# The memory's first update moved beside the scores, and sixteen more periods with keys, then values, then queries

## The chip, the cores and the metric

The kernel runs on one core of one Trainium2 chip. The metric is the device time of one execution in microseconds; the number given for a kernel is the median of its runs.

## What is computed

x has shape (4, 512, 512), the side input the same, the condition (4, 128). The reference is two residual stages, each behind a bidirectional decayed scan:

```python
y = bi_wkv(x, side, side, w, u, cond)            # scans along the 512 tokens, forward and back
q, k, v = y @ Wq, y @ Wk, y @ Wv                 # 16 heads of 128
for each segment of 128 tokens:                  # 4 segments, state (mem, z) per head
    scores = q k^T / sqrt(128), causal; att_dot = softmax(scores) @ v
    sq, sk = elu(q) + 1, elu(k) + 1
    att_mem = sq @ mem / (sq @ z)
    delta = v - sk @ mem / (sk @ z)
    mem += sk^T @ delta ; z += sum(sk)
    att = beta * att_mem + (1 - beta) * att_dot
x = x + att @ Wo
x = x + fwht(silu(z @ W1^T) * (z @ W3^T)) @ W2^T # z = bi_wkv(x, ...) again
```

The change touches the attention alone.

## The kernel before, in words

The program is one core's, with the order of the work of each engine written out by hand. The projections are float32r matmuls in three terms (high times high, high times low, low times high; the helper `three`, L666 to L668), a step of 512 columns each. The weights' high and low halves lie in a ring of seven slots of `parts` (1 MB a tile, both halves together). The small matmuls and transposes of the attention are plain float32, which the trace shows as two passes each for the 128-column ones of L817, L834, L842, L843 and L862.

The attention runs in 32 periods n = 0 to 31: sample n // 8, pair of heads n % 8. A period computes the attention of its two heads and, between those small steps, the projections for the next period: keys k and queries q of n + 1 (`kq_part`, two head halves j, two parts each), and values v (`v_block`, two token halves, two parts each). Values of a couple of head pairs are computed over two periods. Every fourth period (4, 8, ... 28), a burst, has the output projection `wo` of four periods in it besides.

TensorE's order in an ordinary period n: `turn_k` (transposes of sk, L805), `scores` (L817), `turn_att` of n - 1 (L871), two parts of values into bank G[0], `update(n, 0)` (first update of the memory, L834, into a third of bank Z), values into G[1], `recall(n, 1)` (L842, L843), keys, `turn_p` (L852), `update(n, 1)`, keys, `recall(n, 2)`, `pv` (L862), keys, `update(n, 2)`, queries, `recall(n, 3)`, queries. Period 6 alone (`SWAPPED`) has keys where the others have values, values in the middle and queries last.

ScalarE empties the banks G: `copy_v` (L1914) for values; `copy_kq` (L1880), `relu_kq` (L1898) and `minus_exp` (L1889) for keys and queries. The next block into the same bank waits for the semaphore of the last reader: a_v (value copy), a_km (relu of keys) or a_qm (relu of queries). It also has the softmax exponentials (`exp_s`, L1928), `copy_pt` (L1936) and the copy of kn (L1921). VectorE adds the update to the memory (`memory`, L1322), makes delta, the joins and sigma. GpSimd scales the values (`scale_v`, L2299). The second scans and the Hadamard transform of W2 lie between these steps, in `behind(n, k)`, eight places a period, shared out by costs; HH (L1796) and HO (L1814) are ScalarE's part of the transform.

SyncE loads the weights in the order of `STREAM`, which `weight_stream` builds; a tile goes into the next slot of the ring and its load waits until the tile before in that slot has been used (`wait_used`). `held` keeps the slots of a couple's values until the odd period's part of the list has passed. `PLACE` maps a tile's name to its place in the list, `value_tiles` and `kq_part` find their tiles by it. In an even period that is no burst the values of a couple are loaded once and serve the next period too; behind a burst they are loaded again under the kind w. `fetch_x` loads the next sample's x (xb, four transfers) in periods 10, 18 and 26.

Of the kernel before, what the change touches and what calls it, by code (L numbers as in the profile page):

```python
# [19 lines left out]
NN = NB * NG  # L20
# [69 lines left out]
def is_burst(n):  # L90
    return n % 4 == 0 and n > 0
# [60 lines left out]
RAW = [("k", 0), ("v", 0), ("q", 0), ("v", 1)]  # L152


SWAPPED = 6


def couple(n):

    return n + 2 - n % 2  # L160
# [11 lines left out]
def weight_stream():  # L172
    stream, ends = [], []
    for n in range(NN - 1):
        a = couple(n)
        values = [(value_kind(n), a), (value_kind(n), a + 1)]
        has = a < NN and (n % 2 == 0 or is_burst(n - 1))
        keys = [("k", n + 1), ("q", n + 1)]
        if n == 0:
            stream += keys + values  # L180
        elif n == SWAPPED:
            stream += keys[:1] + values + keys[1:]
        else:
            if has:
                stream += values
            if is_burst(n):
                stream += [("o", 8 * (n // 4 - 1) + i) for i in range(8)]
            stream += keys
        ends.append(len(stream))
    ends.append(len(stream) + 3)  # L190
    stream += [("1", 0), ("3", 0)] + [("o", 8 * 7 + i) for i in range(8)] + [("2", 0)]
    for g in range(1, 2 * NG):
        stream += [("1", g), ("3", g), ("2", g)]
    return stream, ends
# [118 lines left out]
def adaln_attn_ffn(nc, xT_d, fT_d, wu_d, wq_d, wk_d, wv_d, wo_d, betas_d,  # L313
# [9 lines left out]
    with ExitStack() as ctx:  # L323
# [338 lines left out]
        def tensor(e):  # L662
# [56 lines left out]
            def v_block(n, half, part):  # L719
                i, k = value_tiles(n)  # L720
                if part == 0:
                    wait_split(w, i)
                    wait_split(w, k)
                    wait_y(couple(n) // NG)
                    if n == 0:
                        w.wait_ge(a_qm, 2 + half + 1)
                    elif n == 1:
                        w.wait_ge(a_v, 2 + blocks_by(0, half))
                    elif n == SWAPPED:
                        w.wait_ge(a_km, 2 * (n + 1) + half + 1)  # L730
                    else:
                        w.wait_ge(a_qm, 2 * n + half + 1)
                b = couple(n) // NG
                rows = slice(128 * tokens_of(n, half), 128 * tokens_of(n, half) + 128)
                x, y = SLOT[i], SLOT[k]
                for c in (0, 1) if part == 0 else (2, 3):
                    hi, lo = (parts[:, p, x:y + 1:y - x, 256 * c:256 * c + 256] for p in range(2))
                    m = three(G[half][:, :], yh[b % 2][:, c, rows], yl[b % 2][:, c, rows], hi, lo, c == 0, c == NC - 1)
                if part == 1:
                    m.then_inc(pe_v, 1)  # L740

            def kq_part(n, kind, j, part):
                b, i = n // NG, PLACE[kind, n]
                hi, lo = ring(i)
                if part == 0:
                    wait_split(w, i)
                    if kind == "q" and n - 1 == SWAPPED:
                        w.wait_ge(a_v, 2 + blocks_by(n - 1, j))
                    elif kind == "q":
                        w.wait_ge(a_km, 2 * n + j + 1)  # L750
                    elif is_burst(n - 1):
                        w.wait_ge(v_xb, 4 * ((n - 1) // 4 - 1) + j + 3)
                    elif n - 1 == SWAPPED or n == NN - 1:
                        w.wait_ge(a_qm, 2 * (n - 1) + j + 1)
                    elif n > 1:
                        w.wait_ge(a_v, 2 + blocks_by(n - 1, j))
                    if n == 1:
                        w.wait_ge(v_v, j + 1)
                        wait_y(0)
                for c in (0, 1) if part == 0 else (2, 3):  # L760
                    cols = slice(256 * c + 128 * j, 256 * c + 128 * j + 128)
                    m = three(G[j][:, :], hi[:, cols], lo[:, cols], yh[b % 2][:, c, :], yl[b % 2][:, c, :],
                              c == 0, c == NC - 1)
                if part == 1:
                    m.then_inc(pe_k if kind == "k" else pe_q, 1)
# [152 lines left out]
            for n in range(NN):  # L918
# [3 lines left out]
                scores(n)  # L922
                if n > 0:
                    turn_att(n - 1)
                bare = n in (0, NN - 2)
                if n in (SWAPPED, NN - 2):
                    kq_part(nx, "k", 0, 0)
                    kq_part(nx, "k", 0, 1)
                elif more and not bare:
                    v_block(n, 0, 0)  # L930
                    v_block(n, 0, 1)
                elif not more:
                    w.wait_ge(a_qm, 2 * n + 2)
                    up(0, 0, "1", G[0])
                if n == 0:
                    kq_part(nx, "k", 0, 0)
                update(n, 0)
                behind(n, 1)
                if more:
                    if n in (SWAPPED, NN - 2):  # L940
                        kq_part(nx, "k", 1, 0)
                    elif not bare:
                        v_block(n, 1, 0)
                    if burst:
                        v_block(n, 1, 1)
                else:
                    up(0, 0, "3", G[1])
# [2 lines left out]
                    behind(n, 3)  # L950
                if burst:
                    wo(n // 4 - 1, 0)
                elif n == SWAPPED:
                    kq_part(nx, "k", 1, 1)
                    v_block(n, 0, 0)
                elif more:
                    if not bare:
                        v_block(n, 1, 1)
                    if n < NN - 2:
                        kq_part(nx, "k", 0, 1 if bare else 0)  # L960
# [6 lines left out]
                if burst:  # L967
                    wo(n // 4 - 1, 1)
                elif bare:
                    kq_part(nx, "k", 1, 0 if n == 0 else 1)  # L970
                elif n == SWAPPED:
                    v_block(n, 0, 1)
                elif more:
                    kq_part(nx, "k", 0, 1)
                else:
                    w.wait_ge(v_f1, 1)
                    up(0, 1, "1", G[0])
                recall(n, 2)
                pv(n)
                if burst:  # L980
                    wo(n // 4 - 1, 2)
                    wo(n // 4 - 1, 3)
                elif n == SWAPPED:
                    v_block(n, 1, 0)
                    v_block(n, 1, 1)
                elif more:
# [718 lines left out]
        def scalar(e):  # L1705
# [311 lines left out]
            for n in range(NN):  # L2017
# [21 lines left out]
                    split_hi(o + 2 if burst else end + 1 if n == 3 else end - 1 if more else end)  # L2039
                exp_s(n, 1)  # L2040
                behind(n, 1)
                if n in (SWAPPED, NN - 2):
                    behind(n, 2)
                    copy_kq(nx, "k", 0, G[0])
                    exp_kq(nx, "k", 0, G[0])
# [9 lines left out]
                    copy_v(n, 1)  # L2055
                split_hi(o + 3 if burst else 3 if n == 0 else end if more else end + 1)
                behind(n, 3)
                if n == SWAPPED:
                    copy_kq(nx, "k", 1, G[1])
                    exp_kq(nx, "k", 1, G[1])  # L2060
                elif more and not bare and not burst:
# [11 lines left out]
                if burst:  # L2073
                    split_hi(o + 8)
                elif more:
                    if n == SWAPPED:
                        copy_v(n, 0)
                    elif n < NN - 2:
                        copy_kq(nx, "k", 0, G[0])
# [2 lines left out]
                behind(n, 5)  # L2082
                if burst:
                    split_hi(end)
                elif n == SWAPPED:
                    copy_v(n, 1)
                elif more:
                    copy_kq(nx, "k", 1, G[1])
# [608 lines left out]
```

## Time and profile before

| | us |
|---|---|
| median of 3 runs | 1576.99 (1576.73 to 1577.36) |
| the profiled execution | 1576.35 |
| its span | 1574.5 |
| TensorE busy | 1540.2 (98%) |
| VectorE busy | 1228.3 (78%) |
| ScalarE busy | 781.2 (50%) |
| GpSimd busy | 613.7 (39%) |
| bytes moved by DMA | 276.58 MB |

The span is the time from the first to the last instruction of the profiled execution; what lies around it is 1.85 us. The granted clock of TensorE was 0.998 over the execution. Periods are told by the first matmul of L805: period 9 starts at 344.17 us, 10 at 370.27, 11 at 396.37, 12 at 422.53, 18 at 623.69 and 25 at 852.04. A time of day in a row is in us from the span's start. Matmuls overlap, so the price of a group is read from start to start, not from the durations. A DMA is issued on SyncE's queue (SPq) and lands later; the time to landing counts from the issue.

### The profile page before, as it was taken

Reading aid. Unit: us, or ns where it says so; the run is one execution under the profiler, and the core shown is the slowest. Engines: PE = TensorE matmul, PEld = TensorE weight load, DVE = VectorE, ACT = ScalarE, POOL = GpSimd, SP = SyncE. Lnnn points to the kernel's source line nnn. Section 1 sums busy time; section 2 is a strip of 40 time slices with the busy share of each in tenths; the row PEclk is TensorE's granted clock in tenths of the full one; section 3 lists DMA queues with packets and bytes.
Section 4 is the critical chain, followed back from the end, with each engine's and each line's share of the span. In section 5 each row is a group of like instructions: output and inputs, shape, how many; then the busy total and the mean of one; then the engine's idle time right before and its main releaser. Section 6 shows DMA issues by size and latency. Waiting matters only on the chain.

```text
span 1574.5 us, 24552 instructions
## 1 busy us (share of the span) xinstructions
PE 1540.2 (98%) x8406; PEld 1321.9 (84%) x8406; DVE 1228.3 (78%) x2746; ACT 781.2 (50%) x1687; POOL 613.7 (39%) x433
## 2 busy tenths in 40 slices
PE   4999999999999999999999999999999999999999
PEld 2788988888888888888888888888888888888887
DVE  8879968898888788898765764776897888677785
ACT  3566656545625526544555562663554443444442
POOL 3656657252111212222001010144664466666662
PEclk9999999999999999999999999999999999999999
DMA  5366677586584486386288559247211221311111
GB/s 177 120 229 238 236 266 277 186 330 245 188 309 159 157 315 233 116 290 226 75 301 312 200 213 335 92 168 260 81 54 57 72 80 68 107 54 54 54 41 54
DMA packets 113405, 276.58 MB, mean 176 GB/s; under 512 B 11648, under 2 KB 36608, under 8 KB 111872
## 3 DMA queue, kind: packets, MB, share of 16 engines
q1 hardware_dynamic: 94416, 241.96, 42.6%
q10 hardware_dynamic: 18864, 33.04, 6.8%
q8 instruction: 68, 1.11, 0.3%
q14 instruction: 57, 0.47, 0.1%
HBM read 226.71 MB, written 48.25 MB: 175 GB/s over the span
## 4 chain that ended last, share of the span: by engine, by line
PE 91%; DVE 5%; issue 2%; ACT 1%; POOL 0%; DMA 0%; ACTq 0%; SPq 0%; DVEq 0%; POOLq 0%
PE psG L666 14%; PE psG L668 14%; PE psG L667 14%; PE psG L790 6%; PE psX L862 4%; PE psX L666 3%; PE psX L667 3%; PE psX L668 3%; PE psX L817 3%; PE psG L792 3%; PE psZ L843 3%; PE psZ L834 3%; PE psZ L667 2%; PE psY L667 2%; PE psZ L666 2%
## 5 line engine op out<-in xcount | busy, mean ns | idle before, releaser
L2231 POOL TENSOR_TENSOR parts<-stage,parts 128x512 fp32r<-128x512 f32 x160 | 234.5, 1487 | 136.2 <-ACT parts L1722 133.7
L666 PE MATMUL psG<-yh,parts 128*128 128x512 f32 x646 | 263.0, 407 | 0.1
L668 PE MATMUL psG<-yh,parts 128*128 128x512 f32 x646 | 253.1, 392 | 0.0
L667 PE MATMUL psG<-yl,parts 128*128 128x512 f32 x646 | 251.9, 390 | 0.0
L2299 POOL TENSOR_TENSOR vs<-v,omb 128x512 f32<-128x512 f32 x64 | 92.9, 1472 | 386.1 <-PE psX L817 210.9
L668 PEld LDWEIGHTS psG<-yh,parts 128*128 128x128 f32 x646 | 121.3, 188 | 26.7
L666 PEld LDWEIGHTS psG<-yh,parts 128*128 128x128 f32 x646 | 121.7, 188 | 22.2 <-issue 0.9
L667 PEld LDWEIGHTS psG<-yl,parts 128*128 128x128 f32 x646 | 121.8, 189 | 21.4
L790 PE MATMUL psG<-heads,parts 128*128 128x512 f32 x384 | 135.5, 394 | 0.0
L1722 ACT ACTIVATE parts<-stage 128x512 fp32r<-128x512 f32 x152 | 88.0, 623 | 50.4 <-DMA stage<-in_w 16.4
L1880 ACT ACTIVATE kT<-psG 128x512 f32<-128x512 f32 x62 | 37.0, 596 | 149.0 <-PE psG L668 147.5
L792 PE MATMUL psG<-heads,parts 128*128 128x256 f32 x384 | 108.2, 282 | 0.0
L1227 DVE RECIPROCAL DBK<-DF 128x128 f32<-128x128 f32 x120 | 107.3, 926 | 0.6
L1928 ACT ACTIVATE S<-S,st 128x128 f32<-128x128 f32 x256 | 99.1, 391 | 7.9 <-issue 5.5
L666 PE MATMUL psG<-parts,yh 128*128 128x512 f32 x240 | 100.4, 418 | 0.0
L1310 DVE CUSTOM_DVE_ANT_0 S<-psX,mask 128x128 f32<-128x128 f32 x256 | 57.9, 286 | 49.4 <-PE psX L817 49.3
L1322 DVE TENSOR_TENSOR mem<-psZ,mem 128x129 f32<-128x129 f32 x192 | 47.8, 287 | 60.1 <-PE psZ L834 60.1
L668 PE MATMUL psG<-parts,yl 128*128 128x512 f32 x240 | 94.5, 394 | 0.0
L667 PE MATMUL psG<-parts,yh 128*128 128x512 f32 x240 | 93.4, 389 | 0.0
L2307 POOL TENSOR_TENSOR hl<-sg,hh 128x512 fp32r<-128x512 f32 x36 | 51.1, 1419 | 91.1 <-ACT hh L1978 91.1
L790 PEld LDWEIGHTS psG<-heads,parts 128*128 128x128 f32 x384 | 72.1, 188 | 14.6
L1889 ACT ACTIVATE etmp<-etmp 128x512 f32<-128x512 f32 x126 | 79.6, 632 | 3.9
(281 smaller groups left out, 4144.5 us busy)
## 6 DMA issues: line engine op xcount, KB each, us to landing
parts<-high_o SPq DMA_DIRECT2D x52, 512.0 KB, 6.0
parts<-low_o SPq DMA_DIRECT2D x52, 512.0 KB, 7.2
parts<-high_v SPq DMA_DIRECT2D x36, 512.0 KB, 5.2
parts<-low_v SPq DMA_DIRECT2D x36, 512.0 KB, 6.6
stage<-in_w SPq DMA_DIRECT2D x64, 256.0 KB, 3.4
parts<-high_k SPq DMA_DIRECT2D x23, 512.0 KB, 5.6
parts<-low_k SPq DMA_DIRECT2D x23, 512.0 KB, 6.7
parts<-high_q SPq DMA_DIRECT2D x23, 512.0 KB, 5.0
```

What stands on the lines that cost most here:

```text
L666: e.matmul(out, lh, rh, start=first, stop=False, skip_group_check=check)
L667: e.matmul(out, lh, rl, start=False, stop=False, skip_group_check=check)
L668: return e.matmul(out, ll, rh, start=False, stop=last, skip_group_check=check)
L790: e.matmul(out[:, :], hi[:, cols], heads[:, :, 8 * half + r, :], start=half == 0 and r == 0, stop=last_row, skip_group_check=True)
L792: k = e.matmul(out[:, 0:256], lo[:, cols], heads[:, 0, 8 * half + r, :], start=False, stop=last_row, skip_group_check=True)
L862: m = e.matmul(X[j][:, seg(s)], pT[:, j, seg(s)], vs[:, s, j, :], start=True, stop=True)
L1227: e.reciprocal(dbk[:, 128 * j:128 * j + 128], df[:, 128 * j:128 * j + 128]).then_inc(v_rc, 1)
L1722: e.activation(hi, raw, ACT.Copy).then_inc(a_wh, 1)
L1889: e.activation(below(n, kind, j), below(n, kind, j), ACT.Exp, scale=-1.0).then_inc(a_ke if kind == "k" else a_qe, 1)
L1928: m = e.activation(S[:, j, seg(s)], S[:, j, seg(s)], ACT.Exp, bias=st[:, 1, j, s:s + 1], scale=-1.0, accum_out=st[:, 2, j, s:s + 1])
L2231: e.tensor_tensor(lo, raw, hi, ALU.subtract).then_inc(p_wl, 1)
L2299: e.tensor_tensor(vs[:, :, j, :].rearrange("p (a b) d -> p a b d", a=2), pick(v[:, :, :, j, 0:P], *HALVES[n]), omb[:, 128 * j:128 * j + 12 ...
```

## The change

`SWAPPED` becomes a rule, `keys_first(n)`, true for period 6 and for the sixteen periods 9, 10, 11, 13, 14, 15, 17, 18, 19, 21, 22, 23, 25, 26, 27 and 29. All places that asked for period 6 ask it. `update(n, 0)` moves for n > 0 from behind the first block to behind `turn_att`. In the list of weights a period with keys first reads key, value, value, query; and the branch that lists them has no question whether the period before has listed the same values (`has`), so that the odd periods 11, 15, 19, 23 and 27 list them a second time.

```diff
-SWAPPED = 6
+def keys_first(n):
+
+    return n == 6 or n > 8 and not is_burst(n) and n < NN - 2
...
         if n == 0:
             stream += keys + values
-        elif n == SWAPPED:
+        elif keys_first(n):
             stream += keys[:1] + values + keys[1:]
         else:
             if has:
                 stream += values
...
# v_block
-                    elif n == SWAPPED:
+                    elif keys_first(n):
                         w.wait_ge(a_km, 2 * (n + 1) + half + 1)
...
# kq_part
-                    if kind == "q" and n - 1 == SWAPPED:
+                    if kind == "q" and keys_first(n - 1):
                         w.wait_ge(a_v, 2 + blocks_by(n - 1, j))
...
-                    elif n - 1 == SWAPPED or n == NN - 1:
+                    elif keys_first(n - 1) or n == NN - 1:
                         w.wait_ge(a_qm, 2 * (n - 1) + j + 1)
...
# tensor, the loop over the periods
                 scores(n)
                 if n > 0:
                     turn_att(n - 1)
+                    update(n, 0)
                 bare = n in (0, NN - 2)
-                if n in (SWAPPED, NN - 2):
+                if keys_first(n) or n == NN - 2:
                     kq_part(nx, "k", 0, 0)
                     kq_part(nx, "k", 0, 1)
...
                 if n == 0:
                     kq_part(nx, "k", 0, 0)
-                update(n, 0)
+                    update(n, 0)
                 behind(n, 1)
...
# scalar, the loop over the periods
-                if n in (SWAPPED, NN - 2):
+                if keys_first(n) or n == NN - 2:
                     behind(n, 2)
                     copy_kq(nx, "k", 0, G[0])
                     exp_kq(nx, "k", 0, G[0])
...
-                if n == SWAPPED:
+                if keys_first(n):
                     copy_kq(nx, "k", 1, G[1])
                     exp_kq(nx, "k", 1, G[1])
```

The other lines of the diff put `keys_first(n)` where `n == SWAPPED` stood, in the same loops of TensorE and ScalarE.

TensorE, period 10, around the first update, before: the values (psG from yh and parts, yh held still) run on both sides of L834.

```order
L667 MATMUL psG<-parts,yh 128x512
L668 MATMUL psG<-parts,yl 128x512
L834 MATMUL psZ<-v,kn 128x129 x2
L666 MATMUL psG<-parts,yh 128x512
L667 MATMUL psG<-parts,yh 128x512
```

And now, from the start of the period:

```order
L807 MATMUL psY<-ident,sk 128x128 x6
L819 MATMUL psX<-kT,qT 128x128 x8
L873 MATMUL psY<-ident,pT 128x128 x8
L836 MATMUL psZ<-v,kn 128x129 x2
L668 MATMUL psG<-yh,parts 128x512
```

The update stands behind the transposes, and the block that follows is keys (yh streams past held weights) where it was values.

ScalarE, the end of period 11's exponentials up to the transposed probabilities, before:

```order
L1928 ACTIVATE S,st<-S,st 128x128 x8
L1914 ACTIVATE v<-psG 128x2x2x128
L1734 ACTIVATE EU<-EU,wu 128x512
L1914 ACTIVATE v<-psG 128x2x2x128
L1936 ACTIVATE pT<-psY 128x512 x2
```

And now:

```order
L1931 ACTIVATE S,st<-S,st 128x128 x8
L1883 ACTIVATE kT<-psG 128x512
L1901 ACTIVATE etmp<-psG 128x512
L1892 ACTIVATE etmp<-etmp 128x512
L1737 ACTIVATE EU<-EU,wu 128x512
L1883 ACTIVATE kT<-psG 128x512
L1901 ACTIVATE etmp<-psG 128x512
L1892 ACTIVATE etmp<-etmp 128x512
L1939 ACTIVATE pT<-psY 128x512 x2
```

Two value copies have become two key copies with a relu and an exponential each; the value copies stand behind pT.

SyncE's queue from the key tile of period 12 on (asked for in period 9 or 10), before:

```order
L2471 DMA parts<-low_k 128x1024
L2509 DMA xb<-in_xT 128x512 x4
L2470 DMA parts<-high_q 128x1024
L2471 DMA parts<-low_q 128x1024
L2470 DMA parts<-high_v 128x1024
L2471 DMA parts<-low_v 128x1024
L2470 DMA parts<-high_v 128x1024
L2471 DMA parts<-low_v 128x1024
L2470 DMA parts<-high_o 128x1024
```

And now:

```order
L2474 DMA parts<-low_k 128x1024
L2512 DMA xb<-in_xT 128x512 x4
L2473 DMA parts<-high_v 128x1024
L2474 DMA parts<-low_v 128x1024
L2473 DMA parts<-high_v 128x1024
L2474 DMA parts<-low_v 128x1024
L2473 DMA parts<-high_q 128x1024
L2474 DMA parts<-low_q 128x1024
L2473 DMA parts<-high_v 128x1024
L2474 DMA parts<-low_v 128x1024
L2473 DMA parts<-high_v 128x1024
L2474 DMA parts<-low_v 128x1024
```

The first two value tiles of the new order are the second copies of those of period 10, and the burst's own values come behind the query tile, two tiles later than before. The queue has 459 rows in place of 439.

## Rows read from the trace of the kernel before

**Rows 1.** The page: the span and the first part, busy us, share, instructions.

```profile
span 1574.5 us, 24552 instructions
...
PE 1540.2 (98%) x8406; PEld 1321.9 (84%) x8406; DVE 1228.3 (78%) x2746; ACT 781.2 (50%) x1687; POOL 613.7 (39%) x433
```

**Rows 2.** TensorE's waits over the span: releaser, us in all, times, longest.

```profile
PE psX L688 <- DVE oys L1233: 23.7, 3, 17.4
...
PE psZ L842 <- DVE mem L1322: 1.1, 4, 0.5
PE psZ L834 <- DVE t L1341: 1.0, 2, 0.8
PE psY L852 <- ACT S L1928: 0.8, 1, 0.8
```

**Rows 3.** Periods 6 and 10: us, busy PE, PEld, DVE, ACT, POOL; clock, DMA.

```profile
243.37:269.47 26.10, 26.10 (x160) 22.99 (x159) 22.11 (x63) 15.85 (x40) 17.63 (x15) 1.00 0.84 287
370.27:396.37 26.10, 26.10 (x160) 22.99 (x159) 21.76 (x65) 15.62 (x39) 6.11 (x5) 1.00 0.32 118
```

**Rows 4.** Timeline of TensorE, periods 11 and 12: start us, us, what.

```profile
402.19 0.40 PE L668 MATMUL psG<-parts,yl 128*128 128x512 f32 x1
402.43 0.61 PE L834 MATMUL psZ<-v,kn 128*128 128x129 f32 x4
402.79 0.47 PE L666 MATMUL psG<-parts,yh 128*128 128x512 f32 x1
403.11 0.39 PE L667 MATMUL psG<-parts,yh 128*128 128x512 f32 x1
403.34 0.40 PE L668 MATMUL psG<-parts,yl 128*128 128x512 f32 x1
...
422.53 0.82 PE L805 MATMUL psY<-ident,sk 128*128 128x128 f32 x6
...
425.77 0.48 PE L666 MATMUL psG<-parts,yh 128*128 128x512 f32 x1
```

**Rows 5.** SyncE's issues in period 11, and landings (KB, us) of the 408.11 and 409.33 issues.

```profile
406.80 0.32 SPq L2470 DMA_DIRECT2D parts<-high_v  x1
...
408.11 0.43 SPq L2471 DMA_DIRECT2D parts<-low_o  x1
...
409.33 0.45 SPq L2471 DMA_DIRECT2D parts<-low_o  x1
...
416.32 0.32 SPq L2470 DMA_DIRECT2D parts<-high_o  x1
...
parts<-low_o SPq DMA_DIRECT2D x1, 512.0 KB, 7.6
parts<-low_o SPq DMA_DIRECT2D x1, 512.0 KB, 9.4
```

**Rows 6.** Periods 10 and 18: an issue, its landing, the matmul in the deadline's place.

```profile
370.82 0.43 SPq L2471 DMA_DIRECT2D parts<-low_v  x1
parts<-low_v SPq DMA_DIRECT2D x1, 512.0 KB, 8.5
380.44 0.40 PE L666 MATMUL psG<-yh,parts 128*128 128x512 f32 x1
...
624.25 0.44 SPq L2471 DMA_DIRECT2D parts<-low_v  x1
parts<-low_v SPq DMA_DIRECT2D x1, 512.0 KB, 9.2
633.87 0.40 PE L666 MATMUL psG<-yh,parts 128*128 128x512 f32 x1
```

**Rows 7.** Timeline of ScalarE and TensorE in period 25.

```profile
860.70 0.60 ACT L1914 ACTIVATE v<-psG 128x512 f32<-128x512 f32 x1 [0.40 <-ACT HO L1814]
861.20 1.05 ACT L1796 ACTIVATE HH<-HA 128x1024 fp32r<-128x1024 f32 x1
...
863.15 0.40 PE L666 MATMUL psG<-yh,parts 128*128 128x512 f32 x1
```

**Rows 8.** A stretch of period 17, columns as in rows 3.

```profile
620.00:622.00 2.00, 2.00 (x10) 1.62 (x9) 1.97 (x8) 0.85 (x2) 1.87 (x1) 1.00 0.05 15
```

More of the change, by code:

```diff
@@ L952, in tensor @@
                     wo(n // 4 - 1, 0)
-                elif n == SWAPPED:
+                elif keys_first(n):
                     kq_part(nx, "k", 1, 1)
@@ L970, in tensor @@
                     kq_part(nx, "k", 1, 0 if n == 0 else 1)
-                elif n == SWAPPED:
+                elif keys_first(n):
                     v_block(n, 0, 1)
@@ L982, in tensor @@
                     wo(n // 4 - 1, 3)
-                elif n == SWAPPED:
+                elif keys_first(n):
                     v_block(n, 1, 0)
@@ L2041, in scalar @@
                 behind(n, 1)
-                if n in (SWAPPED, NN - 2):
+                if keys_first(n) or n == NN - 2:
                     behind(n, 2)
@@ L2075, in scalar @@
                 elif more:
-                    if n == SWAPPED:
+                    if keys_first(n):
                         copy_v(n, 0)
@@ L2084, in scalar @@
                     split_hi(end)
-                elif n == SWAPPED:
+                elif keys_first(n):
                     copy_v(n, 1)
```

## The prediction, made before the changed kernel had run

> **What bounds the kernel now.** I read the page's totals first, then TensorE's waits, then the periods one by one, and last the single rows around the places that the change touches.
>
> The totals show TensorE busy for 1540.2 of 1574.5 us, with VectorE far behind it [rows 1]. The waits of TensorE say where the rest is: 23.7 us before the first period, and then almost nothing. Of the waits behind it, those of the attention periods, the largest group is 1.1 us in four pieces, the next 1.0 and 0.8 us [rows 2]. So in the thirty-two periods TensorE is the bound, and a reordering can win only the few tenths it waits, or what the order itself costs inside TensorE. Period 6 already runs in the new order, keys, values, queries. It lasts 26.10 us with TensorE busy for all of it, as does period 10 in the old order [rows 3]. The new order alone is therefore worth nothing where nobody is late. The question is what it makes late.
>
> **The first update.** update(n, 0) moves ahead of the first weight-sized block in periods 1 to 31. Its two matmuls (four passes) now stand behind the transposes of turn_att, which are plain float32 like them, and no longer between float32r matmuls. What it waits for (kn, the values, t2 of the period before) turn_att has waited for too, or was finished by then. The price today: from L668 at 402.19 to L667 at 403.11 is 0.92 us [rows 4]. Two steps in an undisturbed stretch are 2 x 0.23 = 0.46 us (403.11 to 403.34), so the update costs 0.46 us where it stands. Inside a float32 stretch a pass costs (425.77 - 422.53) / 30 = 0.108 us (6 + 16 + 8 passes of L805, L817, L871), four of them 0.43 us [rows 4]. The move saves 0.03 us a period, **31 x 0.03 = 0.9 us**. Bounds: nothing, if the entry into the next stretch only moves; at most the longer first step of a float32r stretch, 403.11 - 402.79 = 0.32 us against 0.23, so 0.09 us a period and 2.8 us. I take 0.9, since it is read from whole stretches.
>
> The Trainium skill (TensorE: Matmul & The Clock Gate, Part 2, "Single matmul latency") says that a stream of matmuls hides the drain of each, and that a matmul alone pays a constant of about 166 ns. One lone group less in each period would by that page be an estimate of 31 x 0.17 = 5.1 us. The row disagrees: the whole price above what four passes cost is 0.03 us.
>
> VectorE's memory(n, 0) could start earlier. That helps only where VectorE stood ready; where TensorE waits for mem, VectorE was busy with its own queue, and the 1.1 us of rows 2 are all there is. I count nothing.
>
> **Keys, values, queries.** Sixteen more periods take the order of period 6 (9, 10, 11, 13, 14, 15, 17, 18, 19, 21, 22, 23, 25, 26, 27, 29). The number of matmuls is the same. Four things could come late.
>
> (a) ScalarE. v_block(n, 0, 0) now overwrites the bank of the first key half, so it waits for its copy and its relu. Before the copy stands behind(n, 2). The tightest are periods 25 to 27 and 29, where that is the 1.05 us conversion HH. In period 25 the value copy starts at 860.70 and HH at 861.20 [rows 7]. With HH at 860.70 instead, the key copy starts at about 861.7, relu at 862.2, and it ends at 862.8 (0.5 us a step, as from the first row to the second, and 0.6 for the last). TensorE starts the block that takes the place of L666 at 863.15 [rows 7]. It holds by 0.35 us: cost nothing; if a step more comes between, 0.5 us in each of four periods, 2 us.
>
> (b) The ring and SyncE's queue. In the odd periods behind no burst (11, 15, 19, 23, 27) weight_stream now lists the two value tiles again, though the old list had them once for two periods. That is ten tiles, twenty transfers of 512 KB, 10.5 MB more. PLACE keeps the later place of a name, so the even period before also reads the later copy: the first copy is read by nobody and holds two of seven slots. Two deadlines follow.
>
> First deadline: the even periods 10, 14, 18, 22 and 26 wait in v_block(n, 0, 0) for a tile whose slot comes free only when the last query part of the period before ends. The old queue had an issue at just that moment. In period 18 it went out at 624.25 and landed 9.2 us later, at 633.45; TensorE needs it at 633.87: 0.4 us to spare [rows 6]. In period 10: 370.82 + 8.5 = 379.3 against 380.44, 1.1 us to spare [rows 6]. In both the old queue has the same bytes before it, the four loads of xb among them; a key tile is asked for some 9 us later than before, but the transfers sat nearly idle in 620 to 622 (15 GB/s), so it is absorbed [rows 8]. Cost nothing.
>
> Second deadline: before a burst (12, 16, 20, 24, 28) both first value tiles wait for the last v_block of the period before, which now ends where the key part ended, at the issue of 416.32 [rows 5]. The nearest case is the group issued from 406.80 on: its second tile's low half went out at 408.11 and took 7.6 us, 8.9 us after the first issue [rows 5]. So 416.32 + 8.9 = 425.2, while v_block(12, 0, 0) starts at 425.77 + 0.43 = 426.2 [rows 4]. One microsecond to spare, five times. Cost nothing as the value taken. Bound above: if the second tile lands like the third of that group (409.33 + 9.4 = 418.7, 11.9 us after the first issue), each burst starts 2.0 us late [rows 5], 10 us in all.
>
> (c) GpSimd's scaled values for even periods need the value copy, now at about the time of the memory update for which they wait already. No cost. (d) The query parts wait for a_v instead of a_km, one step of ScalarE's less: no cost.
>
> **Sum.** -0.9 us from the update, and a few tenths for deadlines that are missed by little; I put 0.4 us there, one deadline of 0.4 us. The profiled execution took 1576.35 us for its span of 1574.5, 0.64 us under the median of 1576.99, so the difference is set against the median: 1576.99 - 0.9 + 0.4 = **1576.5 us**. A measurement of this kernel tells about 0.2%, 3.2 us, from no change.
>
> **Rivals.** *Forecast: TensorE stays the bound*, within 0.2%. For it: period 6 against period 10, and the empty list of waits.
>
> *Rival A, slower: the weights come late.* The lost prefetch decides: a tile lands over 9.9 us after the first issue before a burst (426.2 - 416.32), or over 9.6 us after its own issue in periods 10, 18 and 26 (633.87 - 624.25). These are eight places. With 0.6 us in each, 1576.99 - 0.9 + 4.8 = 1580.9 us; with 1.2 us in each, 1585.7 us. It counts as slower from 0.5 us a place. Against it: every nearest row lands in time. For it: 0.4 to 1.1 us to spare, while the landing times of rows 5 lie from 7.6 to 9.4 us in one group.
>
> *Rival B, faster: the stretches cost more than I read*, 0.09 us a period (2.8 us), and VectorE, with keys earlier and the update earlier, no longer makes TensorE wait (1.1 us of rows 2): 1576.99 - 3.9 = 1573.1 us. For it: the longer first step in every stretch. Against it: the whole stretches give 0.03. The page of the Trainium skill above (TensorE: Matmul & The Clock Gate) would put it a little lower, at an estimate of 1571.9 us for the drains alone.
>
> *Rival C: ScalarE late* in periods 25 to 29 and with extra operations ahead of the copy: 2 us, 1578.1 us. It stays within 0.2%.
>
> **Numbers.** Forecast and rival C together 0.78 (C 0.08 of it), rival A 0.14, rival B 0.08. The range holds the forecast, C and the near half of A, and of B all but its end: 1574.3 to 1580.9. Faster by over 0.2% has 0.08, no change 0.78, slower 0.14.
>
> **What would show it.** Right: L834 with v directly behind L871, periods 9 to 11 still 26.1 us, burst periods still about 48.2, and TensorE's waits still a few us. The queue of SyncE has twenty issues more and reads 10.5 MB more. Wrong by A: TensorE idle, or "issue" or a DMA named, ahead of the first value block of periods 12, 16, 20, 24, 28, or of the value block in 10, 18, 26. Wrong by B: periods of 26.0 or less everywhere. Wrong by C: L666 behind ACT etmp in periods 25 to 29.

## The result, and the profile after

The changed kernel takes **1578.01 us** (median of 22 runs, 1576.66 to 1580.12) against 1576.20 us (22 runs, 1575.63 to 1577.36) for the kernel before, measured side by side. The ratio is 1.0014, with a 95% interval of 1.0008 to 1.002. The change costs 1.8 us. That is less than the 0.2% that the prediction called no change, and its range (1574.3 to 1580.9) holds the time, but the forecast was a small gain and the kernel became slower by more than the measurement is uncertain. The forecast's base was the median of 3 runs, 1576.99 us, which is 0.8 us above the median of the 22; as a difference it said 0.5 us less, and 1.8 us more were measured. The step that failed is in (b), and it is worth seeing why.

The profiled execution of the changed kernel took 1579.94 us, one of the longer runs, so it shows the loss in full: 3.6 us more than the profiled execution of before. First the totals, as in [rows 1], and the shares of the engines in the chain that ended last:

```profile
span 1578.1 us, 24572 instructions
...
PE 1540.0 (98%) x8406; PEld 1322.4 (84%) x8406; DVE 1228.0 (78%) x2746; ACT 780.7 (49%) x1687; POOL 615.6 (39%) x433
...
PE 89%; DVE 5%; DMA 2%; issue 2%; ACT 1%; POOL 0%; SPq 0%; ACTq 0%; DVEq 0%; POOLq 0%
```

TensorE's busy time is what it was, 1540.0 us, and the span is 3.6 us longer: the loss is idle time of TensorE. The whole kernel's bytes went from 276.58 to 287.07 MB, the 10.5 MB of second copies. In the chain VectorE has 5% and DMA 2%.

The periods say where. Stretches of after from the start of a period to the start of the next (columns as in [rows 3]): periods 10, 12, 13, 18 and 24.

```profile
369.59:396.08 26.49, 26.35 (x159) 22.92 (x158) 21.86 (x65) 15.49 (x39) 6.11 (x5) 1.00 0.47 175
422.21:470.41 48.20, 48.20 (x288) 42.70 (x287) 39.53 (x91) 16.37 (x40) 8.57 (x6) 1.00 0.96 376
470.41:496.48 26.07, 26.07 (x159) 22.99 (x158) 22.65 (x67) 15.08 (x38) 5.60 (x4) 1.00 0.52 180
623.20:649.95 26.75, 26.32 (x159) 22.91 (x158) 20.68 (x63) 15.61 (x39) 7.29 (x5) 1.00 0.47 171
802.87:855.73 52.86, 50.93 (x291) 44.65 (x290) 29.44 (x80) 23.02 (x49) 7.59 (x6) 0.97 1.00 398
```

And of before: periods 12 and 24.

```profile
422.53:470.78 48.25, 48.25 (x288) 42.69 (x286) 39.60 (x91) 16.37 (x40) 8.57 (x6) 1.00 0.80 287
802.87:852.04 49.17, 49.17 (x291) 43.45 (x290) 30.30 (x82) 22.82 (x49) 7.64 (x6) 1.00 0.89 339
```

An ordinary period lasts 26.07 us instead of 26.10, a burst 48.20 instead of 48.25, period 25 26.98 instead of 27.03. Three periods are longer: 10 by 0.39 us, 18 by 0.65 us, and 24 by 3.69 us. At the start of period 24 the two kernels are level (802.87 us in both). Between the first period and this one, 0.64 us had been gained and 1.04 us lost in 10 and 18; that they are level is due to the first period, which began 0.4 us earlier. That start is scatter: it lies between 59.98 and 61.35 us in the profiled executions of all twelve kernels. The one burst behind it makes the result.

**Periods 10 and 18.** Issues and landings of after, two from each period, and the matmul that waits for the second of them (TensorE's timeline):

```profile
370.15 0.48 SPq L2474 DMA_DIRECT2D parts<-low_v  x1
parts<-low_v SPq DMA_DIRECT2D x1, 512.0 KB, 9.9
379.51 0.40 PE L670 MATMUL psG<-yh,parts 128*128 128x512 f32 x1
380.05 0.50 PE L668 MATMUL psG<-parts,yh 128*128 128x512 f32 x1
...
623.76 0.47 SPq L2474 DMA_DIRECT2D parts<-low_v  x1
parts<-low_v SPq DMA_DIRECT2D x1, 512.0 KB, 10.1
633.12 0.40 PE L670 MATMUL psG<-yh,parts 128*128 128x512 f32 x1
633.95 0.48 PE L668 MATMUL psG<-parts,yh 128*128 128x512 f32 x1 [0.43 <-issue]
```

370.15 + 9.9 = 380.05, and 623.76 + 10.1 = 633.86: both value blocks start with the landing. Before, the two loads issued at the same place took 8.5 and 9.2 us [rows 6]. What stands ahead of them has moved: the key tile of period 12 used to be asked for at 355.37 us, and now at 363.38 us, right in front of xb, so xb's first transfer takes 5.4 instead of 4.0 us and the value tile queues behind both.

**Period 24.** This is the chain of after that ended last, through period 24 (start us, us, what):

```profile
821.01 18.23 DMA yh<-ratio_s
...
839.26 0.64 ACT zr L1824
...
839.93 1.29 DVE zr L1261 x2
841.22 0.52 DVE pT L1360 x2
841.74 0.34 DVE xb L1397
...
842.10 0.43 DVE xb L1397
...
842.67 0.47 PE psG L668
```

It begins with a transfer that is no weight: `ratio_s`, one of the two loads of 1 MB each (`z_load`, asked for once in period 24, for the first sample) that feed the scan z. VectorE multiplies what ScalarE makes of it (L1261), and in VectorE's hand-written order this product stands in `behind(24, 5)`, ahead of the last two sums of the output projection (`add_wo`, L1397). Those sums empty bank G, and TensorE's next key block needs the bank. The rows of VectorE and TensorE say the same with their waits, first before (VectorE), then after:

```profile
836.25 1.29 DVE L1258 TENSOR_TENSOR zr<-zr,yh 128x512 f32<-128x512 f32 x2 [3.31 <-ACT zr L1821]
...
840.39 0.88 DVE L1394 TENSOR_TENSOR xb<-xb,psG 128x256 f32<-128x256 f32 x2 [1.53 <-PE psG L792]
```

```profile
839.93 1.29 DVE L1261 TENSOR_TENSOR zr<-zr,yh 128x512 f32<-128x512 f32 x2 [7.04 <-ACT zr L1824]
...
840.13 0.61 PE L836 MATMUL psZ<-delta,kn 128*128 128x129 f32 x4
842.67 0.47 PE L668 MATMUL psG<-yh,parts 128*128 128x512 f32 x1 [1.93 <-DVE xb L1397]
```

VectorE waited 3.31 us for z before, and nobody noticed, since the last output projection still came after it. It now waits 7.04 us. The product starts 3.68 us later, the sums end up last, and TensorE goes from 840.13 to 842.67 in a group whose four passes take 0.36 us when nothing is late: **2.18 us** of waiting. The remaining 1.6 us follow the wait. TensorE's clock in four windows of 2 us (busy, PEclk, DMA share, GB/s):

```profile
840.00:842.00 2.00, 0.74 (x6) 1.00 1.04 414
842.00:844.00 2.00, 1.33 (x4) 0.81 1.02 406
844.00:846.00 2.00, 2.00 (x6) 0.50 1.04 414
846.00:848.00 2.00, 2.00 (x11) 0.84 1.02 408
```

The granted clock falls to 0.50, which is 1.2 GHz, and a step of 512 columns takes 0.43 instead of 0.23 us. The twelve steps from 842.67 take 4.41 us (to 847.08, the L845 behind them) where they take 2.84 in the same place when undisturbed (839.53 to 842.37 in e1, below): 1.57 us. 2.18 + 1.57 = 3.75 us, less the 0.05 us won in this burst as in the others, is the 3.7 us of the period.

Why is z late? The two loads were issued at the same time in both kernels (821.06 and 821.01 us), but before them in the queue lies another amount of data. The landing times of loads issued around 820, of before and then of after:

```profile
parts<-low_k SPq DMA_DIRECT2D x1, 512.0 KB, 7.8
zr<-x_s SPq DMA_DIRECT2D x1, 1024.0 KB, 12.3
yh<-ratio_s SPq DMA_DIRECT2D x1, 1024.0 KB, 14.5
```

```profile
parts<-low_k SPq DMA_DIRECT2D x1, 512.0 KB, 14.0
zr<-x_s SPq DMA_DIRECT2D x1, 1024.0 KB, 16.0
yh<-ratio_s SPq DMA_DIRECT2D x1, 1024.0 KB, 18.2
```

A key tile asked for at 820 us takes 6.2 us longer than before. It is not needed for a long time and lands early enough; z is not so lucky. The transfers that were ahead of it, on SyncE's queue: before, eight were issued from 787.15 to 790.57 and four more up to 803.43; now none of these went out early, and fourteen stand together (first and last):

```profile
796.66 0.32 SPq L2473 DMA_DIRECT2D parts<-high_v  x1
...
804.32 0.45 SPq L2474 DMA_DIRECT2D parts<-low_o  x1
```

That is 7 MB within 8 us. The DMA engines are at their full share (1.00, 398 GB/s) through period 24, so the backlog is still there when z joins it.

The late start of this group alone does no harm, as the kernel without the second copies (e1, below) shows. It too asks for nothing more of this group before 795.70 us, but then for ten transfers only (first and last):

```profile
795.70 0.32 SPq L2473 DMA_DIRECT2D parts<-high_o  x1
...
802.47 0.44 SPq L2474 DMA_DIRECT2D parts<-low_o  x1
```

Its z lands as before. The difference is the burst's own two value tiles, four transfers and 2 MB: e1 had asked for them at 749.52 and 768.35 us, while in the changed kernel two slots held copies that nobody reads, and they joined the crowd. The bytes of the second copies themselves had landed by 755.86 us, 40 us before it.

### The profile page after: what moved, and what is told of

It reads as the page before. It is cut to its first block, busy times and chain, and to the rows that moved or that the text cites. A ratio compares the mean times of both kernels' runs of the same rounds, so it can differ in the third digit from the quotient of the medians.

```text
span 1578.1 us, 24572 instructions
## 1 busy us (share of the span) xinstructions
PE 1540.0 (98%) x8406; PEld 1322.4 (84%) x8406; DVE 1228.0 (78%) x2746; ACT 780.7 (49%) x1687; POOL 615.6 (39%) x433
## 2 busy tenths in 40 slices
DMA packets 116285, 287.07 MB, mean 182 GB/s; under 512 B 11968, under 2 KB 36928, under 8 KB 114752
## 3 DMA queue, kind: packets, MB, share of 16 engines
q8 instruction: 68, 1.11, 0.3%
HBM read 237.19 MB, written 48.25 MB: 181 GB/s over the span
## 4 chain that ended last, share of the span: by engine, by line
PE 89%; DVE 5%; DMA 2%; issue 2%; ACT 1%; POOL 0%; SPq 0%; ACTq 0%; DVEq 0%; POOLq 0%
PE psG L668 14%; PE psG L670 14%; PE psG L669 14%; PE psG L792 5%; PE psX L864 4%; PE psX L668 3%; PE psX L670 3%; PE psX L669 3%; PE psX L819 3%; PE psZ L845 3%; PE psG L794 3%; PE psZ L836 2%; PE psZ L670 2%; PE psY L670 2%; PE psY L669 2%
## 5 line engine op out<-in xcount | busy, mean ns | idle before, releaser
L1917 ACT ACTIVATE v<-psG 128x512 f32<-128x512 f32 x60 | 35.5, 594 | 108.1 <-PE psG L670 106.0
L1883 ACT ACTIVATE qT<-psG 128x512 f32<-128x512 f32 x62 | 37.1, 598 | 95.0 <-PE psG L670 95.0
```

## The experiments

The theory, called L in what follows: the whole loss comes from the second copies in the list, by way of z in period 24 and of one value tile in periods 10 and 18; the update gains 0.03 us a period and the order costs nothing. The rivals: the order itself costs something, the early update takes part in it, or what makes z late is something other than the backlog. In the table, "product" is the start of VectorE's first z product behind the start of period 24, in us; it was read from VectorE's timeline as above.

| kernel | time, us | before beside it | ratio (95%) | period 10 | 18 | 24 | product |
|---|---|---|---|---|---|---|---|
| before, profiled | | | | 26.10 | 26.10 | 49.17 | 33.38 |
| changed | 1578.01 | 1576.20 | 1.0014 (1.0008 to 1.002) | 26.49 | 26.75 | 52.86 | 37.06 |
| e1 listed once | 1575.39 | 1576.34 | 0.9995 (0.9986 to 1.0004) | 26.08 | 26.08 | 49.12 | 33.38 |
| e2 update alone | 1575.74 | 1576.34 | 0.9996 (0.9987 to 1.0005) | 26.08 | 26.07 | 49.12 | |
| e3 order alone | 1578.47 | 1576.34 | 1.0017 (1.0008 to 1.0026) | 26.10 | 26.10 | 50.78 | 36.56 |
| e4 z behind the sums | 1581.99 | 1576.34 | 1.0032 (1.0019 to 1.0044) | 26.42 | 26.08 | 52.73 | |
| e5 first copy read | 1577.69 | 1576.37 | 1.0011 (1.0002 to 1.0019) | 26.08 | 26.08 | 51.40 | 37.18 |
| e6 z a period later | 1578.10 | 1576.37 | 1.0011 (1.0002 to 1.0019) | 26.28 | 26.08 | 49.12 | |
| e7 before + 1 MB | 1577.49 | 1576.37 | 1.0005 (0.9996 to 1.0014) | 26.10 | 26.10 | 50.28 | 36.04 |
| e8 before + 2 MB | 1582.32 | 1576.37 | 1.0037 (1.0023 to 1.0051) | 26.10 | 26.10 | 53.92 | 38.12 |
| e9 order, listed once | 1576.60 | 1576.47 | 0.9999 (0.999 to 1.0008) | 26.10 | 26.10 | 49.18 | 33.36 |
| e10 e1 again | 1576.12 | 1576.47 | 0.9995 (0.9987 to 1.0004) | 26.07 | 26.07 | 49.12 | |

**e1: the second copies taken out of the list.** One line of the changed kernel:

```diff
         elif keys_first(n):
-            stream += keys[:1] + values + keys[1:]
+            stream += keys[:1] + (values if has else []) + keys[1:]
```

> The changed kernel, but the odd periods 11, 15, 19, 23 and 27 list no second copy of their values, so the queue of SyncE has its old 439 rows and all seven slots prefetch. Theory L (the loss is the lost prefetch of the second copies): the late value block in periods 10 and 18 (0.4 and 0.65 us) and the 3.7 us of period 24 are gone, the 0.03 us a period of the early update stays. The attention periods together get about 1 us shorter than before: 1575.2 us against 1576.2, ratio 0.9993. Theory O (the order keys, values, queries itself makes engines late, and the second copies are harmless): period 24 stays above 50 us and the time stays at about 1578.

Measured: 1575.39 us against 1576.34, and all three long periods are gone. Period 24 and the landing of z in it:

```profile
801.91:851.03 49.12, 49.12 (x292) 43.44 (x290) 29.25 (x80) 22.81 (x49) 7.63 (x6) 1.00 0.98 382
```

```profile
zr<-x_s SPq DMA_DIRECT2D x1, 1024.0 KB, 12.3
yh<-ratio_s SPq DMA_DIRECT2D x1, 1024.0 KB, 14.5
```

z lands as before, and TensorE is busy for the whole period. The second copies carry the whole loss.

**e2: the update alone**, the order of the periods left as before (`SWAPPED` again everywhere, `update(n, 0)` behind `turn_att`):

```diff
-def keys_first(n):
-
-    return n == 6 or n > 8 and not is_burst(n) and n < NN - 2
+SWAPPED = 6
```

> The kernel before with the first update behind the transposes in periods 1 to 31, and nothing else. Both theories: 0.03 to 0.04 us less in each of 31 periods, 0.9 to 1.2 us in all: 1575.1 us against 1576.2, ratio 0.9993; period 10 in 26.07 us where it took 26.10. If the gain of the changed kernel's quiet periods comes from the new order and not from the update, this one stays at 1576.2.

Measured: 1575.74 us. Period 9 of it:

```profile
343.94:370.01 26.07, 26.07 (x159) 22.99 (x158) 22.16 (x65) 15.52 (x39) 6.88 (x5) 1.00 1.03 405
```

26.07 against 26.10 us, and 48.19 against 48.25 in burst 12. The move of the update is worth 0.03 us a period, whatever the order around it.

**e3: the order alone**, with its second copies, the update where it stood:

```diff
                 if n > 0:
                     turn_att(n - 1)
-                    update(n, 0)
...
                 if n == 0:
                     kq_part(nx, "k", 0, 0)
-                    update(n, 0)
+                update(n, 0)
                 behind(n, 1)
```

> The changed kernel with the first update back behind the first block: the order of the sixteen periods and the second copies alone. Theory L: the late blocks of periods 10 and 18 and the stall of period 24 as in the changed kernel, without the gain of the update: 1 us more than the changed kernel, about 1579.0 us against 1576.2, ratio 1.0018, the quiet periods back at 26.10. If the early update itself took part in the stall (through VectorE's order), period 24 would be at its old 49.2 us and the time at 1577.

Measured: 1578.47 us. Ordinary periods are back at 26.10, and period 24 lasts 50.78 us: z's loads land 15.5 and 17.6 us after their issue, TensorE waits 1.6 us for the sums, and its clock stays at 1.00. Periods 10 and 18 show no stall here, where I had expected both. That could have meant that the early update has a part in theirs; the landing times, gathered further down, say otherwise.

**e4: VectorE's z product behind the sums.** If only its place in VectorE's order made it harmful, moving the product behind the sums would save the period:

```diff
-                behind(n, 5)
+                if n != 24:
+                    behind(n, 5)
```

> The changed kernel; in period 24 alone VectorE takes the steps of place 5 (the end of a Hadamard level and the products of z, which wait for the 2 MB of x and ratios) behind the sums of the output projection and the joins, not ahead of them. The transfers land as late as in the changed kernel. If the stall of period 24 is VectorE standing in front of z while TensorE waits for the sums: the 2 us before the keys and the half clock behind them are gone, period 24 is near 49.2 us, and only the 1.1 us of periods 10 and 18 are left against the 1 us of the update: 1576.3 us against 1576.2, with a narrow spread, ratio 1.000. If TensorE waits there for the key tile itself: period 24 stays above 51 us and the time at 1578.

Measured: 1581.99 us, worse, and my expectation of 1576.3 missed. The five runs lie between 1578.73 and 1583.10 us, and the profiled one is the fastest of them, so the profile shows at most part of the loss; what the slower runs lost besides stays open. The wait ahead of the key block was gone, and another stood further on. In the waits of this kernel within period 24 it is the only one; behind it, the row of ScalarE:

```profile
PE psG L668 <- ACT etmp L1902: 3.2, 1, 3.2
```

```profile
843.54 3.57 DVE L1261 TENSOR_TENSOR zr<-zr,yh 128x512 f32<-128x512 f32 x4
844.26 1.84 ACT L1829 ACTIVATE yh<-zr 128x512 fp32r<-128x512 f32 x3 [4.37 <-DVE zr L1261]
```

ScalarE has a z step of its own (L1829) ahead of its copy and relu of the keys, and it waits for VectorE's product (4.37 us). What waits for the late load stands in the order of more than one engine, so moving it on one only hands the wait to the next.

**e5: the first copy read, the second one idle.** The bytes, the slots and the times of the issues are those of the change, but the matmuls find the tile that came early (the added wait lets a slot be loaded again only when its idle copy has landed):

```diff
-PLACE = {x: i for i, x in enumerate(STREAM)}
+PLACE = {x: i for i, x in reversed(list(enumerate(STREAM)))}
...
+                    j = BEFORE[i]
+                    if j >= 0 and again(j) and PLACE[STREAM[j]] != j:
+                        w.wait_ge(d_back[SLOT[j]], 32 * fetches(SLOT[j], j + 1))
```

> The changed kernel, but TensorE reads the first copy of a value tile in the even period, and the second copies of 11, 15, 19, 23 and 27 are still loaded and never read. It takes away the late tile of periods 10 and 18 and leaves the twenty transfers and the lost slots. Theory (two separate losses: a tile that comes late in 10 and 18, and a burst that starts with less prefetched): periods 10 and 18 in 26.07 us, period 24 still above 51 us, time 1577 us against 1576.2, ratio 1.0005 to 1.001. If the traffic of the second copies alone delays everything, 10 and 18 stay above 26.3; if it was only the late tile, period 24 is back at 49.1 and the time at 1575.3.

Measured: 1577.69 us. Periods 10 and 18 last 26.08 us, as in e1, and period 24 51.40 us. So there are two separate losses: the late value tile, cured here, and the backlog in front of z, which stays.

**e6: z begun a period later**, on all engines, its loads where they were:

```diff
+                if name == "t0" and i == 0 and n < NN - NG + 1:
+                    break
```

> The changed kernel with the products of z for sample 0, and all second steps behind them, held back until period 25 on every engine. z lands as late as in the changed kernel, and nobody is in front of it before it has. If both VectorE and ScalarE standing before z make the stall: period 24 in 49.1 us, TensorE at full clock throughout, and only the 1.1 us of periods 10 and 18 against the 1 us of the update are left: 1576.3 us against 1576.2, ratio 1.000. If TensorE waits for its own tiles in period 24, it stays above 51 us and the time at 1578.

Measured: 1578.10 us. Period 24 lasts 49.12 us although z lands as late as in the change (15.5 and 17.7 us after issue). The loss of period 24 is thus z's and nothing else's. But the expected 1576.3 us missed, since the steps that moved on came into the periods behind, here 25 (GpSimd is busy for 8.51 us of it, in e1 for 2.54):

```profile
851.35:878.96 27.61, 27.39 (x163) 23.55 (x162) 20.87 (x62) 17.97 (x43) 8.51 (x6) 1.00 0.71 252
```

Periods 25 to 27 lasted 27.4 to 27.6 us instead of 26.98, and 28 lasted 49.44 instead of 49.10. That is 1.9 us together, half of the 3.7 us that period 24 lost in the profile of the change.

**e7 and e8: the backlog by itself.** To the kernel before, with nothing of the change, 1 or 2 MB of extra copies from memory to memory are added to SyncE's queue right ahead of z (two of 512 KB; in e8 four, with the waits at the end adapted):

```diff
                     elif name == "zload":
+                        if i == 0:
+                            for m in range(2):
+                                e.dma_start(extra_s[m], high_s["v"][m]).then_inc(d_o[0], 16)
                         z_load(i)
```

> The kernel before with 1 MB more in SyncE's queue directly ahead of the two transfers of z in period 24: two copies of 512 KB from memory to memory that nobody reads. No second copies, no new order. At the 400 GB/s of that stretch z lands 2.6 us later (before 14.5 us behind its issue). In the changed kernel 3.7 us later cost a wait of 2.2 us, so 1.5 us are free: a wait of about 1.1 us in period 24, 50.2 us where it took 49.2, full clock, 1577.4 us against 1576.2. If the stall needs the new order or the lost slots, this one stays at 1576.2.

> The same with 2 MB (four copies of 512 KB). z lands 5.2 us later, TensorE waits 3.7 us, and the clock falls to half for some 3 us behind the wait as in the changed kernel, which adds 1.5 us: period 24 in 54 us, 1581 us against 1576.2. Without the fall of the clock 1579.9.

Measured: period 24 lasts 50.28 us with 1 MB and 53.92 us with 2 MB. The waits of TensorE, first e7, then e8:

```profile
PE psG L667 <- DVE xb L1395: 0.9, 1, 0.9
```

```profile
PE psG L667 <- DVE xb L1395: 2.9, 1, 2.9
```

The same wait at the same matmul, in a kernel without any of the edits. (By its time alone e7 is not told from before, ratio 0.9996 to 1.0014; the period shows it.) The price of a late product is now readable from three kernels in which the clock stayed at 1.00. In e7, e3 and e5 the period is longer by 1.11, 1.61 and 2.28 us (e5 against 49.12) with the product at 36.04, 36.56 and 37.18: each less its loss leaves 34.93, 34.95 and 34.90. So VectorE could have its product 1.55 us later than before (34.93 - 33.38) without harm, and each microsecond beyond that is one of TensorE's. By this line the change loses 37.06 - 34.93 = 2.13 us (2.18 were read above) and e8 38.12 - 34.93 = 3.19 us. What is left of both is the clock: period 24 of the change is 3.74 us longer than that of e1, so 1.6 us; that of e8 is 4.75 us longer than before, so again 1.6 us. The profiled execution of e8 is 6.1 us longer than that of before; 1.15 us of the rest lie behind the attention, a part that takes between 541.75 and 542.9 us in the twelve profiles, in kernels with and without a loss in period 24.

**e9: the order without the second copies, the update where it stood.**

```diff
-            stream += keys[:1] + values + keys[1:]
+            stream += keys[:1] + (values if has else []) + keys[1:]
...
                     turn_att(n - 1)
-                    update(n, 0)
```

> The new order of the sixteen periods without the second copies, and the first update where it stood before. If the whole loss hangs on the second copies in the list (theory L), the order itself costs nothing: ordinary periods 26.10 us, periods 10 and 18 at 26.1, period 24 at 49.2, z's two loads landing 12 to 15 us after their issue, and a time equal to the kernel before, 1576.2 us within 0.5. If the order costs something of its own (theory O, e.g. a key tile asked for late in an even period), one of the periods 10 to 29 is longer than before by 0.3 us or more and the time is 1577 or above.

Measured: 1576.60 us against 1576.47, ratio 0.9999, periods 26.10 and 49.18. The order of sixteen periods costs nothing and wins nothing.

**e10: e1 once more.**

> The change with the second copies left out, as in the first experiment, measured once more with more rounds. Theory L: the update's 0.03 us a period is all that is left of the change: 0.9 us under the kernel before, some 1575.3 against 1576.2, ratio 0.9994. A rival that the first result was chance: ratio 1.0000 or above.

Measured: 1576.12 us against 1576.47, ratio 0.9995 as in e1. Each interval alone reaches past 1. Three kernels with the early update and without the second copies (e1, e10, e2) all came out at 0.9995 or 0.9996, and their periods are shorter by 0.03 us, so I take a gain of some 0.7 us as likely, not as shown by the times. Against the changed kernel (ratio 1.0008 at least, e1 and e10 1.0004 at most) e1 is the better one.

**The value tile in periods 10 and 18.** The landing times of the load that the value block waits for, in the kernels that wait for it: in period 10 9.3 us (e3), 9.7 (e6), 9.8 (e4) and 9.9 (changed), with the period longer by 0.00, 0.21, 0.35 and 0.42 us than in the kernel with the same update. In period 18 8.6 (e3), 8.9 (e4) and 9.3 us (e6) without loss, and 10.1 us (changed) with 0.68. The loss begins between 9.3 and 9.7 us, where the prediction had put it (9.6).

The other kernels ask for a tile at the same moment, 0.56 us into the period, which nobody waits for there, and its landing time tells what moved it. In period 10 it is 8.4 to 8.9 us in the four kernels with the old order (before, e2, e7, e8) and 9.3 to 10.1 us in all eight with the new one, e9 among them, which has neither second copies nor the early update:

```profile
parts<-low_v SPq DMA_DIRECT2D x1, 512.0 KB, 10.0
```

So in period 10 the new order of the queue brings the tile a microsecond later, and the second copies make TensorE wait for just this tile. The early update has no visible part in it: in e2, which has it with the old order, the tile lands after 8.4 us. In period 18 the two groups overlap, 7.7 to 9.2 us and 8.1 to 10.1 us, and of the four kernels that wait for the tile only the changed one lost anything, so that loss is taken for chance.

## Why the prediction was right or wrong

**What bounds the kernel**: right. TensorE is the bound, and the new order is worth nothing where nobody is late (e9: 26.10 us and a ratio of 0.9999).

**The first update, -0.9 us**: right. 0.03 us a period in ordinary periods and 0.05 in bursts, in the change, in e1 and in e2. The other price for the lone group, an estimate of 5.1 us by the Trainium skill (TensorE: Matmul & The Clock Gate, Part 2, "Single matmul latency"), is not seen: a period in which the group joined the transposes is 0.03 us shorter, not 0.17. The trace disagrees in e2 as it did in the rows of before. That VectorE's memory would gain nothing from it also held: TensorE's waits for `mem` were 1.2 us, four times, against 1.1 [rows 2].

**(a) ScalarE, (c) GpSimd, (d) the query parts, nothing**: right. Periods 25 to 27 last 26.98 us and period 29 27.97 (27.93 before), with no wait behind ScalarE's relu. Rival C did not occur.

**(b), first deadline, nothing**: its place and its point of decision (9.6 us after the issue) were right, its value was a few tenths short. The step was "the transfers sat nearly idle in 620 to 622 (15 GB/s), so it is absorbed" [rows 8]. I took the landing time of before for a load whose neighbours the change had moved. In the changed kernel the same two microseconds carry 189 GB/s, since the key tile and xb are both in flight there. The tile landed after 9.9 and 10.1 us instead of 8.5 and 9.2. Two places, 0.39 and 0.65 us longer, against the 0.4 us of the sum. The order accounts for the later landing in period 10 (9.3 to 10.1 us in eight kernels); in period 18, and in whether the deadline is missed at all, chance takes part (e3 held both, e4 and e6 the second).

**(b), second deadline, nothing at the bursts: this is the step that failed.** The two facts in it were right. Both first value tiles of a burst do wait for the last value block (their issue at 796.66 ahead of burst 24), and they land in time: the last half of the second one 8.1 to 9.1 us after the first issue in the five bursts, against the estimated 8.9, and TensorE starts with them after 9.9 us. But I asked the question for these tiles only, and of TensorE only. The burst's value tiles, 2 MB that could have been loaded tens of microseconds earlier as in e1, went out together with the ten transfers of the output weights. The tiles behind them in the queue had time. What had none was z, 2 MB of another buffer for other engines, which the prediction never names: VectorE had 1.55 us to spare, and z came 3.7 us later. So the missing term is one place, one time: about 2.15 us of waiting and 1.6 us of clock. I asked what a later load makes late next for the weights, and not for the rest of the queue.

**The sum and the rivals.** The profiled execution gives 0.39 + 0.65 + 3.69 us lost and some 0.8 us gained elsewhere up to period 30, 3.9 us, of which 0.4 us is a first period that began earlier. That is the 3.6 us between the two profiled executions. The median loss is 1.8 us. Three kernels with the same list have period 24 at 50.8, 51.4 and 52.9 us (e3, e5, the change), so it is likely, though no second profile of the changed kernel shows it, that most of its runs lose less there than the profiled one, and that its spread of 3.5 us is this. Seven of its 22 runs took 1579.16 us or more, and those may be the ones in which the clock fell. Rival A, the weights come late, was right in its cause (the lost prefetch) and named eight places; two of them lost something. It put the burst's loss at the value block of the burst, where nothing is lost, and it needed 0.6 us in each of eight places where one place with 3.7 us did it.

## What to carry to other kernels

When a change takes prefetch away from a queue, list everything that stands behind the delayed transfers in that queue, also loads for other buffers and other engines, and ask of each engine that waits for one of them what stands behind that wait in its own order. The load that decides is the one with the least time to spare, not the one that was moved. Here the copies that nobody read did their harm by the slots, and so by the time at which other tiles could be asked for; their own bytes had long landed. Ten entries in a list of weights cost more than the 0.03 us a period that the other half of the change gains.

## What the runs showed of the hardware

The granted clock of TensorE is not a matter of how long one pause was. It fell to 0.50 after the pauses of 2.2 us (changed) and 3.2 us (e8), and it stayed at 1.00 after 1.1 us (e7), 1.6 us (e3), 2.3 us (e5) and 3.4 us (e4, from the step at 845.29 to the one at 848.89, less the 0.23 us of a step), the last of them longer than either of the two that were followed by a fall. The fall cost 1.6 us in each of the two. It came 0.6 us after the matmuls had begun again in the changed kernel, and 1.4 us after in e8:

```profile
842.00:844.00 2.00, 0.06 (x1) 1.00 1.05 418
844.00:846.00 2.00, 2.00 (x8) 0.85 1.01 401
846.00:848.00 2.00, 2.00 (x7) 0.50 1.05 418
848.00:850.00 2.00, 2.00 (x11) 0.80 1.00 401
```

TensorE was idle for nearly all of 842 to 844 at a clock of 1.00, and worked at 0.50 only when it had been busy again for 1.4 us. What sets the moment no run here tells.

The other thing is how much a landing time depends on what is in flight. A load of 512 KB on the same queue landed 4.2 us after its issue (the value tile of 787.15, before) and 14.0 us (the key tile of 820.03, after), and the 1 MB of `ratio_s` 14.5 us (before) and 18.2 us (after), with the DMA engines at 405 and 407 GB/s while it was on its way.
